# Graph-transformer block on one core: the ends of the two product phases and the last group's row statistics in another order

## Chip, cores and metric

One core of one Trainium2 chip runs the whole kernel. The metric is the device time of one execution in microseconds (us). A profiled execution also leaves a span (first to last instruction) and the clock that the chip granted TensorE, as a share of full speed (1.00 is 2.4 GHz, 0.50 is 1.2 GHz).

## What is computed

The graph has 1250 nodes of 768 features and 40,000 edges of three relations, sorted by target node. With `ln` a layer norm, the block is:

```python
xn = ln(x)
x1 = x + gnn(xn) + mix(xn)
out = x1 + ffn(ln(x1))
```

`gnn` is two relational graph attention layers, the first with four heads of 192 features, the second with one head of 768 and an `elu` between. One layer is:

```python
xr = einsum('nd,rdf->rnf', x, W)            # one product per relation
qi, kj = xr[etype, dst] @ q, xr[etype, src] @ k
alpha = leaky_relu(qi + kj, 0.2)
e = exp(alpha - segment_max(alpha, dst)[dst])
out = segment_sum(e / segment_sum(e, dst)[dst] * xr[etype, src], dst) + b
```

`mix` is linear attention over all nodes with 12 heads, `ffn` an int8 product whose input is rounded to 8 bits after the layer norm.

## The kernel before

Nodes are held in `NB = 10` blocks of 128 rows, padded to 1280. The edges are never gathered. A table `CT` counts, per relation, source node and target node, how many edges there are (built from one-hot products). The attention weight of a pair of nodes is then a dense value, `exp` of a row term plus a column term, cut by a maximum and multiplied by the count; and `segment_sum` is a dense product of this weight table with `xr`.

Every engine has a stream of its own, written by hand in program order, and they meet only at semaphores: `x.wait_ge(sem, n)` holds up everything behind it on that engine. TensorE (`pe`, PE) multiplies, ScalarE (`act`, ACT) and VectorE (`dve`, DVE) make its operands and clear its banks, GpSimd (`pool`, POOL) makes some operands, SyncE (`sp`, SP) issues all loads and stores of this part in one queue. The work goes through these stages:

- **First-layer products** (`product_steps`, L2091 to L2106). `NE = 80` products of 18 matmuls each, 20 for the mix and 60 for `xr` (three relations, two halves, ten blocks). ScalarE evicts each (`xr_part`, L1079) into one of two buffers `ev[j]`, and SP stores it (`store_product`, `store_xr`) into `xr_d` in the chip's memory, 192 KB each. An eviction waits for its buffer's last store. Masks of the edges and the tables of row maxima (`softmax_tables`, `tq`) are made beside it.
- **Head loop** (L2145 to L2170). For each head, relation and source block one *unit*: ScalarE makes `tb` and `vb` (two exponentials of 128x1260 from the broadcast table `qbc`, `pair`, L1152), VectorE makes `vb` (minimum and maximum, L1688) and `pf` (minimum with a bound, times the count, L1692; both in `weights_pair`, L1681), and TensorE multiplies `pf` with the head's features `xrh` (ten matmuls of two passes, L2153). There are 120 units, of which two buffers `pf[0]`, `pf[1]` are in flight. `load_head(g)` brings one head, 2880 KB; `load_table(i)` brings `qbc`.
- **Second layer.** Between the layers come `elu` and transposes. The second products (`m = 0` to 5, ten blocks each) are evicted by ScalarE into `ev2` (L1211) and its low half by VectorE (L1735), stored by `store_x2` into `x2_d`, and read back as `x2[r]`, block by block for `r = 0`. In the trace these buffers show as `x_d` and `x`. `load_q2(g)` brings the table for group `g`.
- **Group loop** (L2199 to L2212). The targets are worked in `NG = 5` groups of 252. A *step* is two source blocks: VectorE makes `v` and `p` (L1762, L1773), ScalarE the high half `ph` (L1226), GpSimd the low half `pl = p - ph` (`p_low`, L946), TensorE multiplies both with `x2[r]`. Each group has 15 steps.
- **FFN** on the rows `fx`, one block of 126 rows at a time. Row statistics (`row_stats`, L1374, on VectorE) and the reciprocal deviation (`rstd_part`, L870, on GpSimd) of eight of the ten blocks are made inside the last group: `stats_of(ss)` gives four blocks each in steps 3 and 4 of relation 1. In relation 2 the first blocks are quantised.

What sets the order around the change is the place of an instruction in its engine's stream. At the end of the first products SP's stream reads, with product `S1 // PM + 4`, number 70 of 0 to 79:

```python
            sp.wait_ge(mt_tr, NW)
            load_head(sp, 0)
            sp.wait_ge(t_step, 14)
            sp.dma_start(tq_d..., tq[0:NW, :, :, :]...).then_inc(tq_st, 16)
            store_product(S1 // PM + 4)
            sp.wait_ge(tq_st, 16)
            load_table(sp, 0)
            for n in range(S1 // PM + 5, NE):
                store_product(n)
```

VectorE and GpSimd enter the head loop behind `wait_ge(g_done, 12 * NB)`, that is when all of these products are done.

## Time and profile before

| | |
|---|---|
| median of 3 runs | 1714.46 us (1712.40 to 1716.67) |
| profiled execution | 1710.97 us, of it span 1709.2 us |
| granted TensorE clock, mean | 0.972 |
| TensorE busy | 1583.9 us (93%), 10783 matmuls |
| TensorE weight loads (beside the matmuls) | 1145.0 us |
| VectorE busy | 1318.3 us (77%) |
| ScalarE busy | 802.4 us (47%) |
| GpSimd busy | 143.3 us (8%) |
| DMA | 178.55 MB, mean 104 GB/s over the span |

One row of a timeline gives the start from the span's beginning, the duration, the engine, the line of the code, the operation with out<-in, and in brackets how long the engine stood idle before and what it waited for. A row of the waits gives what ended the idle time of an engine: total, number of times, longest. In a window, busy times stand in the order TensorE, its weight loads, VectorE, ScalarE, GpSimd. The granted clock is part of each stretch, so a matmul is longer where it is lower.

### The profile page before, as it was taken

What the parts mean: (1) busy time and instruction counts of PE and PEld (TensorE: products, weight loads), DVE (VectorE), ACT (ScalarE), POOL (GpSimd) and SP (SyncE); (2) the same over time, 40 slices, a digit from 0 to 9 for tenths busy, and PEclk for the clock granted to TensorE, in tenths of its full rate; (3) what the DMA queues carried; (4) which work ended last, traced back from release to release, by engine and by line L of the source; (5) the groups of instructions that cost most, each with busy time, mean ns of one, the idle gap of its engine ahead of it and who ended that gap; (6) DMA issues with size and microseconds to landing.
All of it is one profiled execution on the core that took longest, in us unless ns stands there. A gap on an engine that the chain in (4) does not pass through costs nothing.

```text
span 1709.2 us, 34956 instructions
## 1 busy us (share of the span) xinstructions
PE 1583.9 (93%) x10783; PEld 1145.0 (67%) x10784; DVE 1318.3 (77%) x2641; ACT 802.4 (47%) x1065; POOL 143.3 (8%) x260
## 2 busy tenths in 40 slices
PE   3999998988999999789999999989999799999987
PEld 2566675766556666489999999976555455555544
DVE  8699878999489998088898998972783377777785
ACT  4332114542235654178888888862222233333342
POOL 3000000000000000000000000000000133333340
PEclk8999999999999999989999999989999899999999
DMA  5111115520457663540023033033764621011212
GB/s 188 47 58 59 63 32 182 166 79 28 137 185 221 193 203 100 156 139 31 31 70 113 31 113 104 12 101 95 207 204 142 229 83 55 15 40 55 78 45 91
DMA packets 129214, 178.55 MB, mean 104 GB/s; under 512 B 15429, under 2 KB 100526, under 8 KB 129122
## 3 DMA queue, kind: packets, MB, share of 16 engines
q1 hardware_dynamic: 129122, 177.38, 33.1%
q8 instruction: 51, 0.84, 0.2%
q14 instruction: 41, 0.34, 0.1%
HBM read 120.47 MB, written 56.88 MB: 104 GB/s over the span
## 4 chain that ended last, share of the span: by engine, by line
PE 77%; DVE 9%; issue 5%; ACT 3%; DMA 2%; DVEq 1%; POOL 1%; SPq 1%; ACTq 0%; POOLq 0%
PE ps L2153 22%; PE ps L2105 13%; PE ps L2211 7%; PE ps L2210 7%; PE ps L1911 5%; PE ps L1913 5%; PE ps L1912 5%; PE ps L1924 4%; PE ps L2016 3%; DVE oh_q L1412 1%; PE ps L2222 1%; PE ps L2088 1%; DMA xr_d<-ev 1%; DVE oh_p L1413 1%; PE ps L1967 1%
## 5 line engine op out<-in xcount | busy, mean ns | idle before, releaser
L2153 PE MATMUL ps<-xrh,pf 128*128 (+1 forms) x2400 | 399.6, 329 | 11.9 <-DVE pf L1692 11.9
L2153 PEld LDWEIGHTS ps<-xrh,pf 128*128 128x128 f32 x2400 | 393.1, 191 | 18.5 <-issue 16.5
L1688 DVE SCALAR_TENSOR_TENSOR vb<-vb,tb 128x1260 f32<-128x1260 f32 x120 | 173.0, 1466 | 53.0 <-ACT vb L1162 52.1
L1911 PE MATMUL ps<-w_hi,xt_hi 128*128 128x384 f16 x600 | 198.6, 331 | 15.7 <-issue 8.1
L2210 PE MATMUL ps<-x,ph 128*128 (+1 forms) x600 | 196.2, 327 | 16.5 <-POOL pl L946 10.9
L1692 DVE SCALAR_TENSOR_TENSOR pf<-vb,CT 128x1260 f32<-128x1260 f32 x120 | 175.8, 1468 | 35.1 <-PE ps L2153 35.0
L1912 PE MATMUL ps<-w_lo,xt_hi 128*128 128x384 f16 x600 | 198.2, 330 | 0.0
L1913 PE MATMUL ps<-w_hi,xt_lo 128*128 128x384 f16 x600 | 198.0, 330 | 0.0
L2211 PE MATMUL ps<-x,ph 128*128 (+1 forms) x600 | 197.5, 329 | 0.0
L1412 DVE TENSOR_SCALAR oh_q<-pat,codeT,neg_w 125x630 f16<-125x630 uint16 x420 | 186.8, 445 | 12.0 <-PE ps L1924 7.8
L1162 ACT ACTIVATE vb<-qbc,kcol 128x1260 f32<-128x1260 f32 x120 | 161.0, 1345 | 39.3 <-DVE pf L1692 37.9
L1599 DVE CUSTOM_DVE_ANT_0 tt_junk<-kbc,mb 126x1260 bf16<-126x1260 f32 x120 | 169.1, 1467 | 11.7 <-issue 11.7
L1157 ACT ACTIVATE tb<-qbc,kcol_leak 128x1260 f32<-128x1260 f32 x120 | 159.7, 1343 | 20.5 <-DVE vb L1688 19.0
L1226 ACT ACTIVATE ph<-p 128x252 f16<-128x252 f32 x150 | 61.8, 413 | 163.3 <-PE ps L2211 159.6
L1924 PE MATMUL ps<-oh_q,oh_p 125*128 125x315 f16 x840 | 128.6, 301 | 9.9 <-DVE oh_p L1413 9.5
L946 POOL TENSOR_TENSOR pl<-p,ph 128x252 f16<-128x252 f32 x150 | 112.0, 748 | 223.9 <-ACT ph L1226 212.7
L2105 PE MATMUL ps<-w_hi,xt_hi 128*128 128x384 f16 x360 | 118.5, 329 | 6.7 <-ACT ev L1086 6.7
L2105 PE MATMUL ps<-w_hi,xt_lo 128*128 128x384 f16 x360 | 118.3, 329 | 0.0
L2105 PE MATMUL ps<-w_lo,xt_hi 128*128 128x384 f16 x360 | 118.3, 329 | 0.0
L1924 PEld LDWEIGHTS ps<-oh_q,oh_p 125*128 125x128 f16 x840 | 81.7, 99 | 48.2 <-DVE oh_p L1413 12.3
L1413 DVE TENSOR_SCALAR oh_p<-iota_l,sloT 125x128 f16<-125x128 f16 x420 | 104.9, 250 | 0.0
L1773 DVE SCALAR_TENSOR_TENSOR p<-v,CT 128x252 f32<-128x252 f32 x150 | 69.3, 492 | 45.5 <-ACT v L1218 43.9
(257 smaller groups left out, 2422.9 us busy)
## 6 DMA issues: line engine op xcount, KB each, us to landing
qbc<-tq_d SPq DMA_DIRECT2D x12, 1260.0 KB, 6.4
wst<-in_L_gnn_W SPq DMA_DIRECT2D x60, 192.0 KB, 3.3
xr_d<-ev SPq DMA_DIRECT2D x60, 192.0 KB, 2.1
xrh<-xr_d SPq DMA_DIRECT2D x4, 2880.0 KB, 14.8
x_d<-ev SPq DMA_DIRECT2D x60, 192.0 KB, 2.3
mb_d<-mb SPq DMA_DIRECT2D x30, 310.1 KB
mb<-mb_d SPq DMA_DIRECT2D x30, 310.1 KB
x<-x_d SPq DMA_DIRECT2D x2, 3840.0 KB, 18.9
```

What stands on the lines that cost most here:

```text
L1412: dve.tensor_scalar(oh_q[0:ET, u, :], pat[0:ET, :], codes[:, k:k + 1], neg_w[0:ET, ds(w, 1)], ALU.subtract, ALU.is_equal)
L1599: dve.tensor_tensor_reduce(out=tt_junk[k][0:WK, :], in0=kbc[0:WK, h, :], in1=mb[w % 2][0:WK, :], scale=1.0, scalar=2 * BIG, op0=ALU.subtra ...
L1688: dve.scalar_tensor_tensor(vb[j][:, :], vb[j][:, :], 2.0, tb[j][:, :], ALU.min, ALU.max).then_inc(v_step, 1)
L1692: dve.scalar_tensor_tensor(pf[j][:, 0:ND].rearrange("p (w d) -> p w d", d=WN), vb[j][:, :].rearrange("p (w d) -> p w d", d=WN), 2.0, CT[:, ...
L1911: pe.matmul(ps[:, bank, 0:CW], a_hi, hi[:, k, :], start=(k == 0), stop=False)
L1912: pe.matmul(ps[:, bank, 0:CW], a_hi, lo[:, k, :], start=False, stop=False)
L1913: last = pe.matmul(ps[:, bank, 0:CW], a_lo, hi[:, k, :], start=False, stop=(k == K6 - 1))
L1924: last = pe.matmul(ps[:, bank + q, 0:QH], oh_p[0:ET, u, :], oh_q[0:ET, u, q * QH:(q + 1) * QH], start=start, stop=False, skip_group_check= ...
L2105: mm = pe.matmul(ps[:, 6 + n % 2, 0:CW], a[:, k, i * P:(i + 1) * P], w[:, k, :], start=(q % PM == 0 and c >= C_X), stop=(q % PM == PM - 1))
L2153: mm = pe.matmul(out[b], pf[j][:, b * DB:b * DB + P], x, start=(first and b % 2 == 0), stop=False, skip_group_check=True)
L2210: pe.matmul(ps[:, bank, 0:CW], p, cols(off, off + CW), start=start, stop=False, skip_group_check=True)
L2211: mm = pe.matmul(ps[:, bank + 1, 0:CW + n1], p, cols(off + CW, off + D + n1), start=start, stop=False, skip_group_check=True)
```

## The change

It has three edits.

*End of the first products, start of the head loop.* SP no longer issues `load_head(sp, 0)` ahead of the `tq` store. Six pieces of 480 KB (`load_piece`: one relation, five blocks) follow the stores of products 71 to 76, counted from 0, one behind each. ScalarE makes the four exponentials of the first pair of units behind the evictions of products 74 to 77, into `tb[0]`, `tb[1]` and two new tiles `vb_f`, which lie in the place of the second table `qbc[1]`. VectorE computes this pair once `g_done` is `11 * NB`, not `12 * NB`. SP holds table 1 back until the pair is done (`p_done`), GpSimd writes its constants earlier and in two parts, and TensorE waits for each head's own count (`heads_to`, `one_done`).

*End of the second products.* The blocks of `x2[0]` are loaded two a step during product `m = 4`; before, one a step during 4 and 5. In product 5 SP stores `tq2` and the first pair of blocks before it loads table 0; table 1 is loaded between `x2[1]` and `x2[2]`.

*Last group.* `stats_of(r, ss)` gives two blocks a step: steps 2, 3 and 4 of relation 1 and step 0 of relation 2, before four a step in steps 3 and 4 of relation 1. VectorE's row statistics and GpSimd's `rstd_part` both follow it.

TensorE's stream holds the same matmuls in the same order. Cut to one line of context:

```diff
@@ -232,2 +232,3 @@
         pf = [place(f"pf{j}", [P, ND + 4], F32, 43392 + 5056 * j) for j in range(2)]
+        vb_f = [place(f"vb_f{j}", [P, ND], F32, 105536 + 5056 * j) for j in range(2)]
         he = place("he", [P, NDB, HD + 1], F32, 53760)
@@ -531,2 +532,10 @@
 
+        def load_piece(sp, r, a):
+            sp.dma_start(xrh[0][:, r, a * NB // 2:(a + 1) * NB // 2, 0:HD],
+                         xr_d[0, r, a * NB // 2:(a + 1) * NB // 2, :, :].rearrange("b p n -> p b n")).then_inc(xrh_in[0], 16)
+
+        def heads_to(h):
+
+            return 16 * (h // 2 + 1) + (16 * (2 * R - 1) if h % 2 == 0 else 0)
+
         def bank_of(h, b):
@@ -559,5 +568,6 @@
 
-        def stats_of(ss):
+        def stats_of(r, ss):
 
-            return range(4 * (ss - 3), 4 * (ss - 2)) if ss >= 3 else range(0)
+            b = 2 * (NB // 2 * (r - 1) + ss - 2)
+            return range(b, b + 2) if 0 <= b < NDB - 2 else range(0)
 
@@ -711,3 +721,2 @@
             for j in range(2):
-                sp.wait_ge(ev_out[j], 16 * PW + 16)
                 sp.wait_ge(mb_out[j], 16 * NW // 2)
@@ -715,3 +724,2 @@
             sp.wait_ge(mt_tr, NW)
-            load_head(sp, 0)
             sp.wait_ge(t_step, 14)
@@ -723,2 +731,8 @@
                 store_product(n)
+                k = n - (S1 // PM + 5)
+                if k == 4:
+                    for j in range(2):
+                        sp.wait_ge(ev_out[j], 16 * PW + 16)
+                if k < 2 * R:
+                    load_piece(sp, k // 2, k % 2)
             for j in range(2):
@@ -737,2 +751,4 @@
                         sp.wait_ge(y_exp, (i - 1) * NB)
+                    if i == 1:
+                        sp.wait_ge(p_done, 4)
                     if i >= 1:
@@ -780,3 +796,4 @@
 
-                with sp.Fori(0, NB // 2) as ii:
+                def block_pair(m, ii):
+
                     if M2_0 <= m < M2_0 + 3:
@@ -791,11 +808,18 @@
                         weights_piece2(m + 2, ii)
-                    if m >= M2_0 + 3:
-                        b = NB // 2 * (m - M2_0 - 3) + ii
-                        sp.dma_start(x2[0][:, ds(b, 1), 0:2 * D], x2_d[0, ds(b, 1), :, :].rearrange("b p n -> p b n")).then_inc(x2_in[0], 16)
-                if m == 2 * R - 2:
+                    if m == M2_0 + 3:
+                        for u in range(2):
+                            b = 2 * ii + u
+                            sp.dma_start(x2[0][:, ds(b, 1), 0:2 * D], x2_d[0, ds(b, 1), :, :].rearrange("b p n -> p b n")).then_inc(x2_in[0], 16)
+
+                if m == 2 * R - 1:
                     sp.wait_ge(t_step, 28)
                     sp.dma_start(tq2_d.rearrange("s a (w d) -> w (s a) d", d=WD), tq2[0:NW, :, :, :].rearrange("w s a d -> w (s a) d")).then_inc(tq_st, 16)
+                    block_pair(m, 0)
                     sp.wait_ge(tq_st, 32)
-                    for g in range(2):
-                        load_q2(sp, g)
+                    load_q2(sp, 0)
+                    with sp.Fori(1, NB // 2) as ii:
+                        block_pair(m, ii)
+                else:
+                    with sp.Fori(0, NB // 2) as ii:
+                        block_pair(m, ii)
             for j in range(2):
@@ -805,2 +829,4 @@
                 sp.dma_start(x2[r][:, :, 0:2 * D], x2_d[r].rearrange("b p n -> p b n")).then_inc(x2_in[r], 16)
+                if r == 1:
+                    load_q2(sp, 1)
 
@@ -924,6 +950,14 @@
             last.then_inc(sel_done, 1)
-            pool.wait_ge(g_done, 12 * NB)
+            for j in range(4):
+                pool.wait_ge(oa_out[j], 16 * (2 * NB // 4))
             for j in range(2):
-                pool.memset(xrh[j][:, :, :, HD:HD + 1].rearrange("p r b o -> p (r b) o"), 1.0)
-                pool.memset(pf[j][:, ND:ND + 4], 0.0).then_inc(one_done, 1)
+                pool.wait_ge(mb_out[j], 16 * NW // 2)
+            pool.wait_ge(mk_step, H * NW)
+            pool.wait_ge(mt_tr, NW)
+            pool.wait_ge(g_done, 11 * NB)
+            for j in range(2):
+                pool.memset(pf[j][:, ND:ND + 4], 0.0)
+            pool.memset(xrh[0][:, :, :, HD:HD + 1].rearrange("p r b o -> p (r b) o"), 1.0).then_inc(one_done, 1)
+            pool.wait_ge(g_done, 12 * NB)
+            pool.memset(xrh[1][:, :, :, HD:HD + 1].rearrange("p r b o -> p (r b) o"), 1.0).then_inc(one_done, 1)
 
@@ -953,7 +987,10 @@
                 for r in range(R):
-                    with pool.Fori(1 if g == 0 and r == 0 else 0, NB // 2) as ss:
-                        p_low(g, r, ss)
-                    if g == NG - 1 and r == 1:
-                        for b in range(NDB - 2):
-                            rstd_part(b % 2, NB + b, fmv[:, b, :], frstd[:, b, :], DB)
+                    if g < NG - 1 or r == 0:
+                        with pool.Fori(1 if g == 0 and r == 0 else 0, NB // 2) as ss:
+                            p_low(g, r, ss)
+                    else:
+                        for ss in range(NB // 2):
+                            p_low(g, r, ss)
+                            for b in stats_of(r, ss):
+                                rstd_part(b % 2, NB + b, fmv[:, b, :], frstd[:, b, :], DB)
 
@@ -1125,2 +1162,10 @@
                 xr_part(n)
+                j = n - (NE - 6)
+                if j == 0:
+                    act.wait_ge(qb_in[0], 16)
+                    act.wait_ge(w_lo_done, C_2)
+                if 0 <= j < 2:
+                    act.activation(tb[j][:, :], qbc[0][:, 1, :], ACT.Exp, bias=kcol_leak[:, j, 0:1]).then_inc(y_exp, 1)
+                elif 2 <= j < 4:
+                    act.activation(vb_f[j - 2][:, :], qbc[0][:, 0, :], ACT.Exp, bias=kcol[:, j - 2, R * H:R * H + 1]).then_inc(x_done, 1)
 
@@ -1179,3 +1224,3 @@
                     else:
-                        with act.Fori(0, NB // 2) as ss:
+                        with act.Fori(1 if i == 0 else 0, NB // 2) as ss:
                             pair(i, ss)
@@ -1632,3 +1677,2 @@
 
-            dve.wait_ge(g_done, 12 * NB)
             dve.sem_inc(v_step, 2)
@@ -1680,3 +1724,3 @@
 
-            def weights_pair(i, ss):
+            def weights_pair(i, ss, vb=vb):
 
@@ -1699,3 +1743,6 @@
                     if h == 0:
-                        with dve.Fori(0, NB // 2) as ss:
+                        if r == 0:
+                            dve.wait_ge(g_done, 11 * NB)
+                            weights_pair(0, 0, vb_f)
+                        with dve.Fori(1 if r == 0 else 0, NB // 2) as ss:
                             weights_pair(i, ss)
@@ -1842,11 +1889,10 @@
                             weights_part(g, r, ss)
-                            for b in stats_of(ss) if r == 1 else quantised_in(ss):
-                                if r == 1:
-                                    if b % 4 == 0:
-                                        dve.wait_ge(fx_in[b // 4], 16)
-                                    row_stats(fx[:, b, :], b % 2, NB + b, fmv[:, b, :], DB)
-                                else:
-                                    if b == 0:
-                                        dve.wait_ge(mm_done, U2 + ((NG - 1) * R + 2) * NB + 2)
-                                    quantise(b)
+                            for b in stats_of(r, ss):
+                                if b % 4 == 0:
+                                    dve.wait_ge(fx_in[b // 4], 16)
+                                row_stats(fx[:, b, :], b % 2, NB + b, fmv[:, b, :], DB)
+                            for b in quantised_in(ss) if r == 2 else ():
+                                if b == 0:
+                                    dve.wait_ge(mm_done, U2 + ((NG - 1) * R + 2) * NB + 2)
+                                quantise(b)
                     if r == 0 and g >= 1:
@@ -2142,4 +2188,2 @@
 
-            pe.wait_ge(one_done, 2)
-
             def unit_products(n, h, r, s, j, first):
@@ -2156,3 +2200,5 @@
             for h in range(H):
-                pe.wait_ge(xrh_in[h % 2], 16 * (h // 2 + 1))
+                pe.wait_ge(xrh_in[h % 2], heads_to(h))
+                if h < 2:
+                    pe.wait_ge(one_done, h + 1)
                 if h >= 2:
```

SP's queue around the head's load. `ev` are the eviction buffers, `xrh_188` is `xrh[0]`, `qbc_190` is `qbc[0]`. Before:

```order
L488 DMA xr_d<-ev_144 128x2x192
L529 DMA xrh_188<-xr_d 128x30x192
L718 DMA tq_d<-tq 30x24x42
L488 DMA xr_d<-ev_143 128x2x192
L526 DMA qbc_190<-tq_d 128x2x1260
L488 DMA xr_d<-ev_144 128x2x192
L488 DMA xr_d<-ev_143 128x2x192
L488 DMA xr_d<-ev_144 128x2x192
```

and now:

```order
L489 DMA xr_d<-ev_144 128x2x192
L726 DMA tq_d<-tq 30x24x42
L489 DMA xr_d<-ev_143 128x2x192
L527 DMA qbc_190<-tq_d 128x2x1260
L489 DMA xr_d<-ev_144 128x2x192
L534 DMA xrh_188<-xr_d 128x5x192
L489 DMA xr_d<-ev_143 128x2x192
L534 DMA xrh_188<-xr_d 128x5x192
L489 DMA xr_d<-ev_144 128x2x192
L534 DMA xrh_188<-xr_d 128x5x192
L489 DMA xr_d<-ev_143 128x2x192
L534 DMA xrh_188<-xr_d 128x5x192
```

The load of 128x30x192 is gone from the front; the `tq` store and the table stand behind one store each, and pieces of 128x5x192 alternate with the stores behind them.

ScalarE's stream at the evictions of products 73 to 79 of the first layer, as it is now (before, these seven evictions stood in a row and the exponentials behind them):

```order
L1123 ACTIVATE ev_144<-ps 128x384
L1123 ACTIVATE ev_143<-ps 128x384
L1168 ACTIVATE tb_194<-qbc_190,kcol_leak 128x1260
L1123 ACTIVATE ev_144<-ps 128x384
L1168 ACTIVATE tb_195<-qbc_190,kcol_leak 128x1260
L1123 ACTIVATE ev_143<-ps 128x384
L1170 ACTIVATE vb_f_198<-qbc_190,kcol 128x1260
L1123 ACTIVATE ev_144<-ps 128x384
L1170 ACTIVATE vb_f_199<-qbc_190,kcol 128x1260
L1123 ACTIVATE ev_143<-ps 128x384
L1123 ACTIVATE ev_144<-ps 128x384
```

The two `tb` and the two `vb_f` (here `_198`, `_199`) now stand between evictions.

VectorE's stream in the last group, from the `p` of relation 1's step 3 on before, and of its step 2 now. `stat`, `fmv` are the row statistics of `fx`. Before:

```order
L1773 SCALAR_TENSOR_TENSOR p_0_210<-v_0_208,CT 128x252
L1773 SCALAR_TENSOR_TENSOR p_1_211<-v_1_209,CT 128x252
L1377 BN_STATS stat<-fx 126x6 x2
L1379 MEMSET tick 128x1
L1380 BN_AGGR fmv<-stat 126x2
L1377 BN_STATS stat<-fx 126x6 x2
L1379 MEMSET tick 128x1
L1380 BN_AGGR fmv<-stat 126x2
L1377 BN_STATS stat<-fx 126x6 x2
L1379 MEMSET tick 128x1
L1380 BN_AGGR fmv<-stat 126x2
L1377 BN_STATS stat<-fx 126x6 x2
```

and now:

```order
L1820 SCALAR_TENSOR_TENSOR p_0_212<-v_0_210,CT 128x252
L1820 SCALAR_TENSOR_TENSOR p_1_213<-v_1_211,CT 128x252
L1422 BN_STATS stat<-fx 126x6 x2
L1424 MEMSET tick 128x1
L1425 BN_AGGR fmv<-stat 126x2
L1422 BN_STATS stat<-fx 126x6 x2
L1424 MEMSET tick 128x1
L1425 BN_AGGR fmv<-stat 126x2
L1809 TENSOR_SCALAR v_0_210<-qb_0_208,kcol_leak 128x252
L1811 SCALAR_TENSOR_TENSOR v_0_210<-qb_0_208,kcol,v_0_210 128x252
L1809 TENSOR_SCALAR v_1_211<-qb_0_208,kcol_leak 128x252
L1811 SCALAR_TENSOR_TENSOR v_1_211<-qb_0_208,kcol,v_1_211 128x252
```

Two blocks stand between steps where four did, and the next step's `v` follows them.

## Rows read from the trace of the kernel before

**Rows 1.** Page, part 1 (busy us, share, instructions) and clock of part 2.
```profile
PE 1583.9 (93%) x10783; PEld 1145.0 (67%) x10784; DVE 1318.3 (77%) x2641; ACT 802.4 (47%) x1065; POOL 143.3 (8%) x260
...
PEclk8999999999999999989999999989999899999999
```

**Rows 2.** Waits of TensorE, 695 to 745 us: in total, times, longest.
```profile
PE ps L2153 <- DVE pf L1692: 8.8, 1, 8.8
PE ps L2105 <- ACT ev L1086: 6.7, 2, 5.1
```

**Rows 3.** Waits of TensorE, 1315 to 1360 us.
```profile
PE ps L2210 <- DMA x<-x_d: 5.6, 1, 5.6
PE ps L1911 <- DVE ev L1735: 4.4, 1, 4.4
```

**Rows 4.** Waits of TensorE, 1612 to 1675 us.
```profile
PE ps L2210 <- POOL pl L946: 8.2, 5, 4.2
```

**Rows 5.** Timeline of SP's queue, 668 to 745: start, us, line, transfer.
```profile
687.72 0.36 SPq L529 DMA_DIRECT2D xrh<-xr_d  x1
688.13 6.67 SPq L718 DMA_DIRECT2D tq_d<-tq  x1
```

**Rows 6.** Timeline of ScalarE, 668 to 745: start, us, operation, idle before.
```profile
690.82 0.49 ACT L1086 ACTIVATE ev<-ps 128x384 f32<-128x384 f32 x1 [2.44 <-PE ps L2105]
...
723.33 0.49 ACT L1086 ACTIVATE ev<-ps 128x384 f32<-128x384 f32 x1 [2.44 <-PE ps L2105]
```

**Rows 7.** Windows: busy us of PE, PEld, DVE, ACT, POOL; PEclk, DMA, GB/s.
```profile
259.80:262.00 2.20, 2.20 (x25) 1.48 (x26) 1.93 (x5) 2.02 (x4) 1.15 (x3) 0.50 1.02 376
1616.00:1624.00 8.00, 8.00 (x51) 4.79 (x50) 6.51 (x14) 2.79 (x9) 2.35 (x4) 1.00 0.91 342
1633.30:1637.20 3.90, 3.81 (x24) 2.34 (x24) 3.73 (x16) 0.00 (x0) 3.59 (x10) 1.00 0.00 0
```

**Rows 8.** Chain of waits, 650 to 860: start, us, what.
```profile
732.00 100.62 PE ps L2153 x600
```

**Rows 9.** Page, part 6: transfer, count, KB each, us to landing.
```profile
qbc<-tq_d SPq DMA_DIRECT2D x12, 1260.0 KB, 6.4
```

**Rows 10.** Timeline of VectorE, 668 to 745.
```profile
730.38 2.85 DVE L1692 SCALAR_TENSOR_TENSOR pf<-vb,CT 128x1260 f32<-128x1260 f32 x2
...
737.92 1.47 DVE L1692 SCALAR_TENSOR_TENSOR pf<-vb,CT 128x1260 f32<-128x1260 f32 x1 [1.64 <-PE ps L2153]
```

**Rows 11.** Timeline of TensorE, 259 to 262 and 1623 to 1665.
```profile
259.79 0.17 PE L1987 MATMUL ps<-qk_hi,wt_hi 128*128 128x8 f16 x1 [3.12 <-DVE wt_lo L1509]
...
1633.39 0.33 PE L2210 MATMUL ps<-x,ph 128*128 x1 [1.91 <-POOL pl L946]
...
1637.16 0.33 PE L2211 MATMUL ps<-x,pl 128*128 x1
1641.68 0.48 PE L2210 MATMUL ps<-x,ph 128*128 128x384 f16 x1 [4.19 <-POOL pl L946]
```

**Rows 12.** Timelines of ScalarE and GpSimd, 1285 to 1400.
```profile
1319.22 0.49 ACT L1211 ACTIVATE ev<-ps 128x384 f16<-128x384 f32 x1 [2.43 <-PE ps L1913]
...
1348.89 0.49 ACT L1211 ACTIVATE ev<-ps 128x384 f16<-128x384 f32 x1 [2.43 <-PE ps L1913]
...
1350.83 1.46 POOL L946 TENSOR_TENSOR pl<-p,ph 128x252 f16<-128x252 f32 x2 [31.05 <-ACT ph L1226]
```

**Rows 13.** Timeline of VectorE, 1605 to 1650.
```profile
1620.50 1.05 DVE L1773 SCALAR_TENSOR_TENSOR p<-v,CT 128x252 f32<-128x252 f32 x2 [0.74 <-ACT v L1218]
...
1625.41 1.00 DVE L1377 BATCH_NORM_STATS2 stat<-fx 126x6 f32<-126x384 f32 x2
...
1632.38 1.01 DVE L1377 BATCH_NORM_STATS2 stat<-fx 126x6 f32<-126x384 f32 x2
...
1636.95 0.30 DVE L1762 TENSOR_SCALAR v<-qb,kcol_leak 128x252 f32<-128x252 f32 x1
```

2 lines of the change are left out of this document (1 added, 1 removed).

## Prediction

> **What bounds the kernel now.** I read the page first: TensorE is busy for 1583.9 of 1709.2 us, and its granted clock is in the top tenth nearly everywhere [rows 1]. So time comes back only where TensorE stands still or runs slowly, and the reader should look for such places next to the edits. The waits of TensorE show three. Around the end of the first layer's products it waits 8.8 us for the first weights `pf` and 6.7 us for evictions [rows 2]. At the end of the second layer's products it waits 5.6 us for a load and 4.4 us for an eviction [rows 3]. In the last group of the second layer it waits 8.2 us in five pieces for `pl` [rows 4]. The engine and queue timelines then say what each wait hangs on.
>
> **Edit 1, end of the first product.** Before, the 2880 KB load of head 0 is issued at 687.72, and everything behind it in SP's queue is late: the issue of the next store alone takes 6.67 us [rows 5]. The evictions wait for their buffers' stores. ScalarE evicted one product per 2.93 us (0.49 + 2.44) up to 690.82; eight more would have ended at 690.82 + 8 x 2.93 = 714.3, but the last one starts at 723.33 [rows 6]. That is 9.1 us: 6.7 idle, the rest, as I take it, a spell at the lower clock behind it. After the change the load comes in six pieces of 480 KB, one behind each of six stores. A product then brings 192 + 480 KB = 0.69 MB per 2.93 us, 235 GB/s, where a busy stretch carried 342 GB/s [rows 7]. I cost the pieces at nothing for that reason; what hides them is that third of the rate left over, and if it goes, evictions are late again (rival 1). The sixth piece is issued at about 706.3 and has 8 us to land. **Gain 9.1 us**; bounds 0 and 9.1.
>
> The product of the weights moves too. Before, from the last eviction (723.33) to the first matmul of the head loop (732.00 [rows 8]) run two pairs of exponentials, two minima and the first `pf`: 8.67 us. Now ScalarE makes the four exponentials of the first pair behind the evictions of products 74 to 77, each about 1.35 us in a 2.44 us hole, so no eviction is late. ScalarE's new wait for the table sits in front of evictions 75 to 79, which PE waits for. The table goes out once `tq` has been stored, at 688.5 to 692, and takes 6.4 us [rows 9]: 695 to 698.5, against product 74's eviction at 699.6. The fourth exponential ends at 710.2, and one minimum and one product of 1.47 us each put `pf0` at 713.2, 1 us before TensorE is free. So unit 0 starts at 714.3 with no wait and units 0 and 1 fill until 720.8: 30 units take 100.62 us [rows 8], unit 0 of them about 5.85 since VectorE's next `pf` waits for it until 737.92 [rows 10], the others (100.62 - 5.85) / 29 = 3.27. The 8.67 us chain now starts at 714.3 and feeds **unit 2**, at 722.9; TensorE idles 2.1 us in between. Before, unit 2 started at 737.85 + 3.27 = 741.1. Everything of edit 1 together: 741.1 - 722.9 = **18.2 us**. It contains the 2.6 us that unit 0 lost at the lower clock. Whether 2.1 us idle brings that clock back is not certain; after 1.91 us idle the granted clock was 1.00 [rows 7, 11], so I charge nothing and keep 2.6 us as a bound. Then VectorE works 2.94 us a unit against TensorE's 3.27, so the lead is kept. The load that is moved stands behind the `tq` store, a store and the table in SP's queue, all three wanted sooner than it. SP's new wait for the first two `pf` (714.6) has only table 1 behind it, wanted at unit 10, 30 us later. GpSimd's new waits have two short memsets behind them and then nothing until the head loop ends. All of these cost nothing while the head loop's own lead of that size stands.
>
> **Edit 2, end of the second product.** Two 756 KB table loads stood in front of the stores of product pair 0, and the eviction at 1319.22 was the last in time: eight intervals to 1348.89 should be 23.4 us and are 29.7 [rows 12]. The first load now goes behind the pair's two stores, where the next store is due in 2.9 us, and the second leaves the stretch. **Gain 6.3 us**, bounds 0 and 6.3. The blocks of `x2[0]` load two per step during product 4, 768 KB and 384 KB of stores in 5.85 us, about 200 GB/s, covered as above. TensorE no longer waits for the last block but for `pl`: two take 1.46 us from 1350.83, so the first is there at 1351.6, where TensorE started at 1354.4 (last eviction 1348.89 plus 5.6) [rows 3, 12]. **Gain 2.8 us**. It still idles 2.8 us. At 3.12 us idle the clock behind it was 0.50 [rows 7, 11], at 1.91 us 1.00; 3.12 is nearer, so I leave the clock loss of about 1.6 us as it is; it is the upper bound's extra. The loads of `x2[1]` and `x2[2]` go out earlier by the same shift; table 1 slips in between and is wanted 60 us later.
>
> **Edit 3, row statistics.** VectorE did four blocks at a time: 1632.38 to 1636.95 is 4.57 us, so two cost 2.28; one step of weights in a dense stretch is 1632.38 - 1625.41 - 4.57 = 2.40 us [rows 13]. A step of TensorE is 1637.16 + 0.16 - 1633.39 = 3.94 us [rows 11], and it starts 1.0 us after VectorE's step ends (1633.39 against 1632.38). With two blocks each, VectorE needs 4.68 against 3.94, so TensorE now loses about 0.8 a step instead of 1.91 and then 4.19. VectorE is free for the first two blocks at 1621.5; the rows of `fx` must have landed. No row says when: not before 1621.5 is of use, and before the change they were read at 1625.41 without a wait. The four transfers of 378 KB and the first 1512 KB load, 3.1 MB at 342 GB/s [rows 7], take 9.1 us, so I take 1623. Then TensorE's steps start at 1628.8, 1633.5, 1638.2 and 1642.9, with idle times of 1.3, 0.8, 0.8 and 0.8 us, and one of 0.3 behind them. Before it was 8.2 us [rows 4], of which I leave 0.7 for the change of groups (1.91 and 4.19 are in it, so the other three waits are 2.1 together), plus some 1.5 us at the lower clock behind the 4.19 (the two waits of edit 1 cost 2.4 so). **Gain** 7.5 + 1.5 - 4.0 = **5.0 us**, bounds 2.7 (landing at 1625.4, 2.3 us later) and 6.6 (no wait, 1.6 earlier). GpSimd's eight pairs of row statistics spread likewise and stop delaying `pl`.
>
> **Sum.** 18.2 + 6.3 + 2.8 + 5.0 = 32.3 us off the profiled execution's 1710.97: 1678.7. The median of the runs is 3.5 us above that execution, so I say 1714.46 - 32.3 = **1682 us**. With the favourable ends of edits 2 and 3 (1.6 and 1.6 more) it is 1679; with the clock loss in edit 1 (2.6) and the late `fx` (2.3), 1687.
>
> **Rivals.** (1) *The transfers are late*, and the ends of both products still stall. A store behind a 480 KB piece, at half of 342 GB/s, takes 4.0 us with it where 2.93 are free; over six products 1.1 us each, 6.6 us, give 1688.6. For it speaks that stores did queue behind loads in both stretches [rows 2, 3], against it that the old loads were six times a piece. The Trainium skill, DMA: Bandwidth & Descriptors, section Bandwidth, asks for transfers of 1 MiB and more and lists 138 GB/s for 64 KB against 341 for 1 MB; a 480 KB piece lies between, and by that rule the time would be this rival's. The trace carried 342 GB/s with transfers of 378 and 1512 KB mixed, so I give it 0.12. (2) *VectorE is simply full in the last group.* The work is only moved, and if the step with statistics costs the two idle times all the same, edit 3 gives 0: 1687. Chance 0.08. (3) *Slower.* The idle places are also TensorE's rests. If 600 us of products and head loop without one made the chip grant less in the 120 units of the head loop (402 us), the gain is gone at a mean clock of 0.925 there (402 / 0.925 is 33 us more); below that point the kernel is slower, at 0.90 by 45 us more: 1727 us. Against it: the slices that lie wholly in that loop show a 9 [rows 1], and its 29 units after the first keep 3.27 us with no rest. Chance 0.03. (4) *The early weights come too late or the edits miss*: nothing but part of edit 2, within 5 us of before. Chance 0.03.
>
> **How the numbers follow.** The forecast, 1677 to 1687, has 0.74. With rivals 1 and 2 and both together (up to 1693) it is 0.94. The range 1676 to 1691 leaves out the far end of these and rivals 3 and 4. The measurement tells about 0.3% (5 us) from no change. Faster 0.94, same 0.03, slower 0.03.
>
> **What would show it.** In the changed profile: evictions of the last ten first-layer products 2.93 us apart; the first head-loop matmul within 0.5 us of the last product, and one wait for `pf` of about 2 us two units later; no wait of an eviction in the last second-layer product; a wait of about 2.8 us for `pl` in place of 5.6 for the load; in the last group four or five waits under 1.5 us. I am wrong if evictions still wait for stores beside the pieces, if the first `pf` is waited for, or if TensorE's clock in the head loop is under 0.98.

## The result, and the profile after

Median 1687.08 us against 1715.57 before, four runs each. One of the new kernel's four, at 3281.23 us, stands apart for a reason that is not known: it is in that median, but not in the ratio of 0.983 (95% interval 0.9803 to 0.9857). The median of the other three is 1685.57. The forecast was 1682, in the range 1676 to 1691. The gain is 28.5 us by the first median, 30.0 by the second and 29 by the ratio, where 32.3 were worked out. The profiled execution has a span of 1683.7 us, 25.5 less than before. Both kernels spread by 8 to 10 us between executions (the 20 runs of before in one comparison went from 1709.5 to 1719.3), so below the profiles are read for where time goes, and the ratios for how much.

The page after and TensorE's waits over the same three stretches answer to [rows 1 to 4]. The page, busy time and granted clock:

```profile
PE 1579.6 (94%) x10783; PEld 1143.5 (68%) x10784; DVE 1318.7 (78%) x2641; ACT 803.2 (48%) x1065; POOL 143.4 (9%) x260
...
PEclk7999999998999999999999999989999999999998
```

TensorE's waits from 650 to 745 us (in total, times, longest):

```profile
PE ps L2197 <- DVE pf L1736: 2.2, 1, 2.2
```

from 1280 to 1350:

```profile
PE ps L2256 <- POOL pl L980: 2.8, 1, 2.8
```

and from 1580 to 1660:

```profile
PE ps L2256 <- POOL pl L980: 6.7, 6, 3.6
```

The 8.8 and 6.7 us at the end of the first products have become 2.2, the 5.6 and 4.4 at the end of the second have become 2.8, and the 8.2 of the last group are still 6.7. That third line is where the forecast went wrong.

To compare stretches across executions I measure from fixed instructions. `T1` is the eviction of product 71 (690.82 in before, 692.45 in after); `T2` the first matmul of the group loop; `T3` TensorE's matmul behind a wait of 0.62 us in the last group (1615.58 in before, 1589.94 in after), which is where the `fx` loads go out; `T4` the FFN's first matmul with a 2.57 us wait ahead; `T5` the end of the span.

| us | T1 to T2 | T2 to T3 | T3 to T4 | T4 to T5 |
|---|---|---|---|---|
| before | 663.62 | 261.14 | 59.10 | 34.52 |
| after | 636.57 | 260.92 | 57.71 | 36.05 |
| after, profiled again | 637.80 | 262.49 | 57.81 | 35.97 |
| edit 1 alone | 647.17 | 261.21 | 59.20 | 34.47 |
| edit 2 alone | 654.78 | 259.55 | 59.17 | 34.45 |
| edit 3 alone | 663.58 | 261.03 | 55.34 | 34.53 |
| edits 1 and 2 | 638.19 | 260.81 | 58.43 | 34.49 |

From T1 on the changed kernel is 27.1 us shorter. T1 itself came 1.6 us later, with a granted clock of 0.76 in the first 50 us against 0.83, which makes the 25.5 of the span. In the five profiles whose kernels agree up to T2 (the last row, the two of after, and the two further kernels below that change only the last group) T1 to T2 runs from 635.90 to 638.19, so a difference of 2 us in that column says nothing by itself.

**First products.** The chain of waits and VectorE's timeline answer to [rows 8, 10]. The chain (start, us, what):

```profile
680.65 35.10 PE ps L2151 x216
715.75 6.55 PE ps L2197 x40
...
724.51 91.89 PE ps L2197 x560
```

VectorE's timeline:

```profile
713.21 2.85 DVE L1736 SCALAR_TENSOR_TENSOR pf<-vb_f,CT 128x1260 f32<-128x1260 f32 x2
...
722.90 2.84 DVE L1736 SCALAR_TENSOR_TENSOR pf<-vb,CT 128x1260 f32<-128x1260 f32 x2
```

TensorE runs from the products into unit 0 without a stop (680.65 + 35.10 = 715.75), and unit 2's `pf` starts at 722.90. Before, it began unit 2 at 741.1, which is 50.3 us after T1; now it is 724.51 - 692.45 = 32.1 us, 18.2 earlier, just the forecast's 18.2. From 690.0 to 715.7 us, beside the pieces, the DMA engines moved 235 GB/s on average, as much as the forecast had worked out for a store and a piece.

One eviction was nevertheless late, ScalarE's rows:

```profile
695.37 0.49 ACT L1123 ACTIVATE ev<-ps 128x384 f32<-128x384 f32 x1 [2.43 <-PE ps L2151]
699.15 0.49 ACT L1123 ACTIVATE ev<-ps 128x384 f32<-128x384 f32 x1 [3.29 <-DMA xr_d<-ev]
701.22 0.49 ACT L1123 ACTIVATE ev<-ps 128x384 f32<-128x384 f32 x1 [1.58 <-PE ps L2151]
701.61 1.34 ACT L1168 ACTIVATE tb<-qbc,kcol_leak 128x1260 f32<-128x1260 f32 x1
...
715.85 0.49 ACT L1123 ACTIVATE ev<-ps 128x384 f32<-128x384 f32 x1 [2.43 <-PE ps L2151]
```

The eviction at 699.15 waited 3.29 us for the last store of its buffer, some 0.9 longer than the 2.43 of the others, but the next came 2.07 us later and TensorE, with a second bank, never waited. The exponentials fill the holes as costed, 1.34 us in 2.43.

**Second products.** GpSimd's timeline at its first `pl`:

```profile
1328.21 1.46 POOL L980 TENSOR_TENSOR pl<-p,ph 128x252 f16<-128x252 f32 x2 [24.07 <-ACT ph L1271]
```

TensorE's timeline:

```profile
1329.02 0.48 PE L2256 MATMUL ps<-x,ph 128*128 128x384 f16 x1 [2.84 <-POOL pl L980]
```

Two windows, busy times, then granted clock, DMA share and GB/s:

```profile
724.50:728.00 3.50, 3.49 (x21) 3.49 (x22) 3.30 (x3) 3.14 (x3) 0.00 (x0) 1.00 1.10 337
1329.00:1333.00 4.00, 3.98 (x16) 2.01 (x17) 3.21 (x8) 1.24 (x3) 0.80 (x3) 0.64 0.59 152
```

No load is waited for any more; `pl` is, for 2.84 us. In this profile the granted clock is 1.00 behind the 2.23 us of idle time ahead of unit 2 (724.50 to 728), and 0.64 over 4 us behind the 2.84 (1329 to 1333). The last section shows that the second does not hold in every execution.

**Last group.** VectorE and TensorE answer to [rows 11, 13]. VectorE's timeline:

```profile
1594.87 0.97 DVE L1820 SCALAR_TENSOR_TENSOR p<-v,CT 128x252 f32<-128x252 f32 x2 [0.75 <-ACT v L1263]
1599.88 1.02 DVE L1422 BATCH_NORM_STATS2 stat<-fx 126x6 f32<-126x384 f32 x2 [4.05 <-DMA fx<-y_d]
```

SP's queue:

```profile
1589.35 5.42 SPq L849 DMA_DIRECT2D fx<-y_d  x2
```

TensorE:

```profile
1605.54 0.50 PE L2256 MATMUL ps<-x,ph 128*128 x1 [3.63 <-POOL pl L980]
```

VectorE is free at 1595.8 and stands 4.05 us for `fx`, whose load was issued at 1589.35. TensorE then stands 3.63 us for the `pl` behind it, and its next matmuls take 0.50 us each where 0.33 is usual: the granted clock is 0.65 over the next 4 us.

### The profile page after: what moved, and what is told of

Read it like the earlier page. It is cut to its first block, busy times and chain, and to the rows that moved or that the text cites. A ratio compares the mean times of both kernels' runs of the same rounds, so it can differ in the third digit from the quotient of the medians.

```text
span 1683.7 us, 34901 instructions
## 1 busy us (share of the span) xinstructions
PE 1579.6 (94%) x10783; PEld 1143.5 (68%) x10784; DVE 1318.7 (78%) x2641; ACT 803.2 (48%) x1065; POOL 143.4 (9%) x260
## 4 chain that ended last, share of the span: by engine, by line
PE 71%; issue 16%; DVE 8%; ACT 2%; DVEq 1%; DMA 1%; POOL 0%; SPq 0%; POOLq 0%; ACTq 0%
PE ps L2197 22%; PE ps L2151 14%; PE ps L2257 7%; PE ps L2256 7%; PE ps L1970 4%; PE ps L2062 3%; PE ps L1957 2%; PE ps L1958 2%; PE ps L1959 2%; PE ps L2268 1%; DVE oh_q L1457 1%; PE ps L2134 1%; DVE stat L1422 1%; DVE oh_p L1458 1%; PE ps L2013 1%
## 5 line engine op out<-in xcount | busy, mean ns | idle before, releaser
L2197 PEld LDWEIGHTS ps<-xrh,pf 128*128 128x128 f32 x2400 | 390.9, 190 | 11.3 <-issue 8.9
L1970 PE MATMUL ps<-oh_q,oh_p 125*128 125x315 f16 x840 | 127.9, 300 | 10.2 <-DVE oh_p L1458 9.7
L2257 PE MATMUL ps<-x,pl 128*128 (+1 forms) x300 | 98.5, 328 | 0.0
```

What stands on the lines that cost most here:

```text
L1970: last = pe.matmul(ps[:, bank + q, 0:QH], oh_p[0:ET, u, :], oh_q[0:ET, u, q * QH:(q + 1) * QH], start=start, stop=False, skip_group_check= ...
L2197: mm = pe.matmul(out[b], pf[j][:, b * DB:b * DB + P], x, start=(first and b % 2 == 0), stop=False, skip_group_check=True)
L2257: mm = pe.matmul(ps[:, bank + 1, 0:CW + n1], p, cols(off + CW, off + D + n1), start=start, stop=False, skip_group_check=True)
```

## The experiments

Twelve runs followed, of eleven new kernels and the changed one again, in three groups on three chips (the first four, the next four, the last four). The kernel before, run beside each group, had medians of 1712.52, 1712.56 and 1712.15 us, against 1715.57 above. So the ratios to it carry over between groups, and medians do not; where an expectation names a time, the ratio is to be put on 1715.57. The first four runs split the change; the kernel with one edit is the kernel before with that edit's hunks of the diff alone.

**Edit 1 alone.**

> The kernel before with edit 1 alone (pieces of the head's load behind six stores, exponentials and weights of the first pair early). Theory A, the accounting from the two profiles: the edits add up, and edit 1 is worth 18.6 us (head loop ends 16.9 us earlier, and the stretch ahead of the edit had been 1.6 us longer), so about 1697 us against 1715.6. Theory B, the edits lean on each other (later stages lose part of it again, as the last group's wait comes at another moment): less than 15 us, over 1700. In the profile under A: one wait for pf of about 2.2 us two units into the head loop, the last product's eviction to the first unit under 0.3 us.

Median 1694.68, ratio 0.9889 (0.9868 to 0.991): 19 us, theory A. By the table, T1 to T2 falls by 16.5 us. Unit 2 starts 32.1 us after T1 (722.41 - 690.35), as early as in the changed kernel; what is missing from 18.2 lies behind it and is within the spread of that column.

**Edit 2 alone.**

> The kernel before with edit 2 alone (order of transfers at the end of the second products). Theory A: 8.4 us, 6.3 of it the evictions' wait and the rest the load of the last block replaced by the wait for pl; 1707 us. Theory B: under 6 us, 1710 or more. In the profile under A: no wait of an eviction in the last second-layer product, a wait of about 2.8 us for pl at the start of the group loop, and a spell of lower clock behind it.

1704.04, ratio 0.9944 (0.9925 to 0.9964): 9.6 us, theory A; T1 to T2 falls by 8.8. The edits add within the spread: 16.5 + 8.8 = 25.3 against 25.4 with both (663.62 - 638.19).

**Edit 3 alone.**

> The kernel before with edit 3 alone (two blocks of row statistics a step, one step earlier). Theory A, as the two profiles account it: VectorE stands about 4 us for the rows of fx, the last group gains only 1.4 us and the FFN loses 1.5, so 1715.6 within 1.5 us. Theory C, my prediction's price was right and the shortfall lies elsewhere (the start of the kernel, the FFN by chance): 5 us faster, 1710.6. In the profile under A: a wait of TensorE for pl of 3 to 4 us where statistics of the first two blocks are made, and the first fx statistics start about 4 us after their p.

1714.66 (12 runs), ratio 1.0004 (0.9989 to 1.002): nothing that the interval of some 3 us either way can tell. But its profile doesn't show what theory A says: TensorE's longest wait in the last group is 1.7 us. VectorE's timeline:

```profile
1624.60 1.02 DVE L1381 BATCH_NORM_STATS2 stat<-fx 126x6 f32<-126x384 f32 x2 [2.08 <-DMA fx<-y_d]
```

TensorE:

```profile
1630.26 0.33 PE L2213 MATMUL ps<-x,ph 128*128 x1 [1.67 <-POOL pl L947]
```

Here the rows of `fx` landed 8.0 us after T3 (1624.60 - 1616.63), and the last group was 3.8 us shorter, at 1708.24 us for this execution. The runs of this kernel went from 1707.5 to 1718.5. So I take it that what edit 3 brings hangs on a landing time that the median execution doesn't meet; only this one execution was profiled.

**Edits 1 and 2 without 3.**

> The changed kernel with edit 3 undone. Theory A: the same time as the changed kernel within 1.5 us, 1687. Theory C: 5 us slower than it, 1692. The last group should show the waits of before, 1.9 and 4.2 us for pl; whether the FFN's three or four blocks at the lower clock come back as before tells whether its 1.5 us belong to edit 3.

1687.4, ratio 0.9845 (0.9821 to 0.9869): 2.6 us over the changed kernel by the ratios, with intervals that overlap. The last group's two waits are 2.58 and 2.63 us here, not the 1.9 and 4.2 expected. The landing varies here too: in this profile and in that of edit 1 alone, VectorE waited 0.6 and 1.3 us for `fx` even one step later, 10.5 and 11.3 us after T3. The FFN took 34.5 us in all five profiles without edit 3.

**One transfer for six pieces.** (`heads_to` follows, with one count for the load in place of six.)

```diff
                 k = n - (S1 // PM + 5)
-                if k == 4:
-                    for j in range(2):
-                        sp.wait_ge(ev_out[j], 16 * PW + 16)
-                if k < 2 * R:
-                    load_piece(sp, k // 2, k % 2)
+                if k == 0:
+                    for j in range(2):
+                        sp.wait_ge(ev_out[j], 16 * PW + 16)
+                    load_head(sp, 0)
```

> The changed kernel, but head 0 is loaded by one transfer of 2880 KB behind the store of product 71, in place of the six pieces. Tests whether it is the pieces that free the evictions, or already that the load no longer stands ahead of the tq store. Theory A (a large transfer holds up the stores behind it, pieces do not): the evictions of products 73 and on wait for their stores again, 5 to 9 us in all, and the exponentials of the first pair, which stand between evictions, come late with them; 1693 to 1696 us against 1687. Theory R (the place alone counts): no eviction waits over 1 us, 1687.

ScalarE's timeline:

```profile
700.89 0.49 ACT L1122 ACTIVATE ev<-ps 128x384 f32<-128x384 f32 x1 [3.15 <-DMA xr_d<-ev]
710.28 0.49 ACT L1122 ACTIVATE ev<-ps 128x384 f32<-128x384 f32 x1 [8.90 <-DMA xr_d<-ev]
```

SP's queue:

```profile
695.30 0.44 SPq L530 DMA_DIRECT2D xrh<-xr_d  x1
697.76 24.51 SPq L489 DMA_DIRECT2D xr_d<-ev  x7
```

The DMA view from 690 to 724 us (KB, us to landing):

```profile
xrh<-xr_d SPq DMA_DIRECT2D x1, 2880.0 KB, 14.4
```

1689.71, ratio 0.9865 (0.9842 to 0.9889). One eviction waited 8.9 us for the last store of its buffer and TensorE 4.9 us for that eviction; T1 to T2 is 641.95, 4.8 over the mean of the two profiles of after. The load was issued at 695.30 and landed 14.4 us later, at about 709.7; the store issued behind it at 697.76 released the eviction at 710.28. So a store behind a 2880 KB transfer landed only with it. That is theory A; the time, 1692.4 if the ratio is put on 1715.57, falls just short of its 1693. By the profiles the pieces are worth about 5 us, by the ratios 6, with intervals that overlap. The rest of the 9.1 us that edit 1 was to gain on the evictions would then come with the order in the queue, the `tq` store and the table ahead of the load; this was not run by itself.

**The first pair late.** The pieces stay; ScalarE's and VectorE's first pair stand behind the products again.

```diff
-                j = n - (NE - 6)
...
-                if 0 <= j < 2:
-                    act.activation(tb[j][:, :], qbc[0][:, 1, :], ACT.Exp, bias=kcol_leak[:, j, 0:1]).then_inc(y_exp, 1)
...
-                            dve.wait_ge(g_done, 11 * NB)
-                            weights_pair(0, 0, vb_f)
-                        with dve.Fori(1 if r == 0 else 0, NB // 2) as ss:
+                            dve.wait_ge(g_done, 12 * NB)
+                        with dve.Fori(0, NB // 2) as ss:
```

> The changed kernel with the six pieces, but the first pair's exponentials and weights back behind the products, as before. By the sum of the prediction edit 1 is 9.1 us for the evictions and the rest, 18.2 - 9.1 = 9.1, for the early pair; so 9 us slower than the changed kernel, 1696, with one wait for pf of 8.8 us ahead of unit 0 and none ahead of unit 2. If the early pair only moves the 8.8 us chain by two units (6.5 us) and the rest came from the clock, the price is 6.5 us, 1693.5.

TensorE's timeline, the start of the head loop:

```profile
723.62 2.59 PE L2188 MATMUL ps<-xrh,pf 128*128 128x193 f32 x7 [8.76 <-DVE pf L1728]
```

1693.48, ratio 0.9894 (0.9873 to 0.9916), 8 us over the changed kernel's 1685.57 and 1685.29 by the medians and 11 by the ratios, with an interval of some 4 us either way. T1 to T2 is 644.36, 7.2 us over the mean of the two profiles of after. The profiles give the early pair about 7 us, which would be the chain of 8.7 moved by two units of 3.27, with little from the clock; the ratios don't exclude the 9.1 of the forecast.

**Pairs unit by unit.**

```diff
+                for j in range(2):
+                    act.wait_ge(v_step, n + j + 1)
+                    act.activation(tb[j][:, :], qbc[i % 2][:, 1, :], ACT.Exp, bias=sub(kcol_leak, 2 * ss + j)[:, a:a + 1]).then_inc(y_exp, 1)
+                    act.wait_ge(p_done, n + j + 1)
+                    act.activation(vb[j][:, :], qbc[i % 2][:, 0, :], ACT.Exp, bias=sub(kcol, 2 * ss + j)[:, R * H + a:R * H + a + 1]).then_inc(x_done, 1)
...
+                            (weights_by_unit if r == 0 else weights_pair)(i, ss)
```

> The changed kernel with the pairs of head 0, relation 0 (from the second pair on) made unit by unit: ScalarE tb0, vb0, tb1, vb1, VectorE vb0, pf0, vb1, pf1. The chain behind the last eviction is then two exponentials and two VectorE operations, 1.35 x 2 + 0.2 + 1.47 x 2 = 5.8 us, and pf of unit 2 is there when TensorE ends unit 1: the wait of 2.2 us goes, 1685. If the unit-by-unit order costs VectorE's lead later in the loop (a wait for pf in pairs 2 to 4), the gain is under 1 us, 1686 to 1688.

VectorE's timeline:

```profile
716.69 1.47 DVE L1756 SCALAR_TENSOR_TENSOR vb<-vb,tb 128x1260 f32<-128x1260 f32 x1 [2.84 <-ACT vb L1204]
718.30 1.47 DVE L1759 SCALAR_TENSOR_TENSOR pf<-vb,CT 128x1260 f32<-128x1260 f32 x1
```

`pf` of unit 2 ends at 719.8, before TensorE ends unit 1 (713.38 + 6.55 = 719.9), and TensorE has no wait over 0.35 us before 746.8, where it is 0.48. 1680.55, ratio 0.9821 (0.9802 to 0.9839). T1 to T2 is 633.95, 3.2 us under the mean of the two profiles of after. The median fell by 5 us against the changed kernel's 1685.57, but by the ratios it is 1.5, with intervals that overlap; put on 1715.57, the ratio gives 1684.9, the 1685 expected.

**The `fx` load in two.**

```diff
-                sp.dma_start(fx[0:DB, 4 * q:4 * q + 4, :], y_d.rearrange("(b p) n -> p b n", p=DB)[:, 4 * q:4 * q + 4, :]).then_inc(fx_in[q], 16)
+                for f0, f1, k in (((0, 2, 0), (2, 4, 1)), ((4, 8, 2),))[q]:
+                    sp.dma_start(fx[0:DB, f0:f1, :], y_d.rearrange("(b p) n -> p b n", p=DB)[:, f0:f1, :]).then_inc(fx_in[k], 16)
...
-                                if b % 4 == 0:
-                                    dve.wait_ge(fx_in[b // 4], 16)
+                                if b in (0, 2, 4):
+                                    dve.wait_ge(fx_in[b // 2], 16)
```

> The changed kernel with the first load of fx (four blocks, 1512 KB) split into two of two blocks, each with a semaphore of its own. Theory D: edit 3 gains little because the first rows of fx land 9.9 us after the anchor (TensorE's short wait in step 1 of relation 1) where they are wanted at 6; half the bytes land some 2 to 3 us earlier, VectorE's wait of 4.05 us falls under 1.5, TensorE's wait of 3.6 under 1.9 and its spell at the lower clock goes: 3 to 4 us faster, 1683.5. Rival: the transfers around it (loads of ac, stores of y, 1.5 MB) set the landing and not its own size: no change, 1687.

VectorE's timeline:

```profile
1594.46 1.02 DVE L1423 BATCH_NORM_STATS2 stat<-fx 126x6 f32<-126x384 f32 x2 [1.86 <-DMA fx<-y_d]
```

TensorE:

```profile
1600.12 0.33 PE L2257 MATMUL ps<-x,ph 128*128 x1 [1.44 <-POOL pl L981]
...
1604.84 0.33 PE L2257 MATMUL ps<-x,ph 128*128 x1 [0.60 <-POOL pl L981]
```

The first two blocks are there 7.7 us after T3 in place of 9.9. VectorE waits 1.86 us, where under 1.5 was expected, and TensorE 1.44; its matmuls behind that wait keep 0.33 us, so the clock stays up. T3 to T4 falls from 57.7 to 55.1. 1681.43, ratio 0.982 (0.9804 to 0.9836), 1.7 us under the changed kernel by the ratios, with intervals that overlap.

**The changed kernel again**, as the baseline of the last three.

> The changed kernel again, unedited, as the baseline on the same chip for the other three. 1685 to 1688. Its FFN stretch tells whether the 36.05 us seen in the first profile (34.5 in five others) belong to the kernel or vary from one execution to the next: theory V, they vary, 33 to 36 here too.

1685.29, ratio 0.9832 (0.9805 to 0.9859). The last group repeats: VectorE waits 4.22 us for `fx`, 10.1 after T3. So does the FFN, 35.97, where theory V wanted it to vary.

**The split without edit 3.**

> Edits 1 and 2, not 3, with the first fx load split in two as in the run before. A control: if edit 3 needs the early rows of fx to pay (theory D), then the split alone, with four blocks a step and one step later, gains at most the 0.6 to 1.3 us that VectorE waited there, 1686 to 1687, and the last group still shows about 1.9 and 4.2 us of waits. If the split pays by itself, 1683, as with edit 3.

TensorE's timeline in the last group:

```profile
1606.42 0.33 PE L2254 MATMUL ps<-x,ph 128*128 x1 [1.92 <-POOL pl L980]
...
1614.71 0.48 PE L2254 MATMUL ps<-x,ph 128*128 128x384 f16 x1 [4.19 <-POOL pl L980]
```

1684.59, ratio 0.9839 (0.9812 to 0.9865). The two waits of before are there again, T3 to T4 is 60.6, 5.5 us over the kernel with edit 3 and the split (4.0 if the 59.1 of before is taken, which is 1.5 less for the same waits). In the profiles this speaks for theory D. So does the time: 0.9839 of 1715.57 is 1687.9. But its interval, 4.5 us either way, all but reaches the 1683 of the other case, and the 3.3 us by the ratios between this kernel and edit 3 with the split lie within intervals that overlap.

**The group loop's first pair early.**

```diff
                     if m == 2 * R - 1:
                         exp_v(0, 0, 0)
-                    x2_hi(m, NB // 2 - 1)
-            p_hi(0, 0, 0)
+                        x2_hi(m, NB // 2 - 1, (0,))
+                        p_hi(0, 0, 0)
+                        x2_hi(m, NB // 2 - 1, (1,))
```

VectorE's `p` (`p_count(0, 0, 0)`) stands between its last two `x2_lo` in the same way.

> The changed kernel with the first pair of the group loop (p, ph, pl) made between the last two evictions of the second products, in place of behind them. TensorE's wait of 2.84 us for pl goes and the lower clock behind it (0.5 to 1.5 us): 3 to 4 us faster, 1683; if step 1 of the loop is late in its place (its ph waits behind the last eviction), a wait of about 1 us appears there and the gain is 2.

TensorE's timeline at the start of the group loop:

```profile
1327.57 0.32 PE L2262 MATMUL ps<-x,ph 128*128 128x384 f16 x1
...
1332.49 0.33 PE L2262 MATMUL ps<-x,ph 128*128 x1 [0.84 <-POOL pl L980]
```

The wait is gone at 1327.57 and one of 0.84 us stands in step 1, as in the second case expected. T1 to T3 is 895.8 us, against 896.5 to 900.3 in the five profiles named under the table. 1683.74, ratio 0.9835 (0.9808 to 0.9862), no difference that these rounds can tell from the baseline's.

**All three together.**

> The changed kernel with all three further edits: pairs of head 0, relation 0 unit by unit (2.5 us by the profiles), fx load split (2.6 us in the last group, and what the clock gives), first group pair early (3 us). They lie in three different stages, so they should add: 8 us, 1678 or ratio 0.977 to before; TensorE's waits in 700 to 1660 us without one over 1.5 us except the two around the FFN.

1673.89, ratio 0.977 (0.9745 to 0.9795), 11.4 us under the changed kernel run beside it by the medians and 10.6 by the ratios, with intervals that do not overlap; 8 us, or a ratio of 0.977, was expected. It is the fastest of the study. T1 to T2 is 631.23, T3 to T4 54.94.

## Why the prediction was right, and where it was off

**Edit 1 was right in size.** Predicted 18.2; measured 16.5 (profile of it alone) to 19 (ratio). Evictions and unit 0 followed the plan, the 2.1 us idle ahead of unit 2 was 2.23 and cost no clock. How it splits is known less well. The early pair was costed at 9.1 (the chain shift 6.5 and the clock behind the old wait 2.6) and gave about 7 by the profiles and 11 by the ratios; by the profiles pieces and order then gave 9 to 10 for the forecast's 9.1. Edits 1 and 2 together were to bring 27.3 us; T1 to T2 fell by 25.4 to 27.7 in the five profiles of both.

**Edit 2 was right.** Predicted 6.3 + 2.8 = 9.1; measured 8.8 and 9.6. The 2.84 us of idle time is the forecast's 2.8.

**Edit 3 failed.** Predicted 5.0 with bounds 2.7 and 6.6; by the ratio of it alone nothing, in the full kernel 2.6 us with overlapping intervals (0.983 against 0.9845), and 1.3 us in its own stretch. The step that failed is "so I take 1623" for the landing of `fx`, 7.4 us after T3. I worked it out as 3.1 MB at 342 GB/s: the two `ac` loads, the two `y_d` stores of 378 KB each and the first half of `fx`. In the changed kernel's profile the four go out at 1586.2 to 1587.9 and the first half at 1589.35. The second half of `fx`, which the sum left out, goes out at 1594.5, 5.4 us before the first half lands at 1599.9. SP's queue:

```profile
1586.24 0.75 SPq L841 DMA_DIRECT2D ac<-acc_d  x2
1587.03 0.83 SPq L567 DMA_DIRECT2D y_d<-ot  x2
```

The DMA view from 1585 to 1610 us, traffic and issues:

```profile
DMA packets 1598, 4.67 MB, mean 187 GB/s; under 512 B 84, under 2 KB 84, under 8 KB 1596
...
fx<-y_d SPq DMA_DIRECT2D x2, 1512.0 KB
ac<-acc_d SPq DMA_DIRECT2D x2, 378.0 KB
y_d<-ot SPq DMA_DIRECT2D x2, 378.0 KB
```

From the first of these issues to the landing (window as before, GB/s last):

```profile
1586.24:1599.88 13.64, 13.02 (x80) 7.66 (x79) 8.34 (x18) 4.77 (x12) 4.77 (x7) 1.00 0.83 277
```

So 4.6 MB share the queues in place of 3.1. Up to the landing 13.64 us at 277 GB/s moved 3.8 MB, and the landing came 2.5 us later than I took. As an estimate, 0.7 MB more at 342 GB/s is 2.0 us of it; a mean rate under 342 is the rest. The landing also varies. In the nine profiles with edit 3, VectorE's first row statistics and the last group go together:

| run | first statistics, us after T3 | T3 to T4 |
|---|---|---|
| all three together | 7.6 | 54.9 |
| `fx` load in two | 7.7 | 55.1 |
| edit 3 alone | 8.0 | 55.3 |
| first pair late | 8.8 | 56.5 |
| after | 9.9 | 57.7 |
| pairs unit by unit | 10.0 | 57.7 |
| after, profiled again | 10.1 | 57.8 |
| group loop's pair early | 10.2 | 57.9 |
| one transfer for six | 11.3 | 59.4 |

Each us of landing costs about 1.2 us, and at 11.3 nothing is left of the gain (59.1 before). The two divided loads are the two earliest, but edit 3 alone came within 0.3 us of them with an undivided one; why the undivided load lands anywhere from 8.0 to 11.3 is open. The rest of edit 3's sum held: with the landing at 7.7, near my 7.4, TensorE's waits for `pl` with the load in two are 1.44, 0.60, 0.53, 0.54, 0.90 and 0.59, 4.6 us together, where I had 4.0 and 0.7 for the change of groups, and the gain is 4.0 of 5.0.

That the rows "were read at 1625.41 without a wait" (9.8 after T3) was no bound to trust either: two profiles without edit 3 landed at 10.5 and 11.3. With 9.9 VectorE is late by 2.5 us more than I took. That is about the landing of my lower bound, 1625.4, and yet the gain is under its 2.7: TensorE's wait is 3.6 us where I had 1.3, and behind it comes a spell at the lower clock (0.65 over 4 us, 1.4 us lost) that the bound did not hold. The gain in T3 to T4 is 59.1 - 57.8 = 1.3 us, and 1.5 us more in the FFN, at the lower clock, take it back in both profiles of after.

**The FFN** was in no term. In all five profiles without edit 3 it took 34.5 us from T4; in the nine with it 33.2 once, 34.5 three times and 36.0 five times. TensorE's wait ahead is 2.57 us in all of them. What differs is how long the clock is down behind it, in windows of 4 us from T4 (the granted clock is the third number from the end). Before:

```profile
1674.68:1678.68 4.00, 4.00 (x13) 2.36 (x14) 3.86 (x8) 1.62 (x2) 0.00 (x0) 0.57 0.41 141
1678.68:1682.68 4.00, 4.00 (x30) 2.78 (x28) 3.40 (x7) 2.28 (x3) 0.00 (x0) 1.00 0.43 149
```

After:

```profile
1647.65:1651.65 4.00, 4.00 (x18) 2.65 (x19) 3.86 (x8) 1.62 (x2) 0.00 (x0) 0.71 0.41 141
1651.65:1655.65 4.00, 4.00 (x15) 2.16 (x14) 2.98 (x6) 2.54 (x3) 0.00 (x0) 0.50 0.43 149
```

Unit by unit:

```profile
1641.42:1645.42 4.00, 3.86 (x23) 2.57 (x24) 3.86 (x8) 1.62 (x2) 0.00 (x0) 1.00 0.41 141
1645.42:1649.42 4.00, 4.00 (x27) 2.61 (x24) 3.93 (x9) 2.54 (x4) 0.00 (x0) 1.00 0.43 149
```

0.57 and 1.00, then 0.71 and 0.50, then 1.00 and 1.00. The same stop costs 0, 1.3 or 2.8 us. Why edit 3's kernels so often get the long spell was not tried; that it goes with the edit is what 5 and 9 profiles show, no more.

**The rivals.** Rival 1 (evictions late beside the pieces) shows as one eviction of 0.9 us delay, without effect; at 2880 KB in one transfer it is true. The Trainium skill's rule of 1 MiB and more per transfer (DMA: Bandwidth & Descriptors, section Bandwidth) did not decide here: six pieces of 480 KB went through without a wait of TensorE, where one transfer of 2880 KB cost it 4.9 us. Rival 2 (edit 3 gives nothing, 1687) came close in number, by another mechanism: not because VectorE is full, since with early rows the same distribution took T3 to T4 down by 3.8 us (edit 3 alone) and 5.5 (with the split load, against the split without edit 3). Rival 3 (lower clock in the head loop) is refuted: the granted clock (third from the end) is 1.00 over it, where under 0.98 was to be the sign.

```profile
716.00:1108.00 392.00, 387.20 (x2341) 380.81 (x2340) 347.20 (x288) 334.52 (x261) 0.00 (x0) 1.00 0.23 72
```

Rival 4 (early weights too late) is refuted too: unit 0 follows the last product without a wait.

So the time fell in the upper part of the range, which "landing at 1625.4" and rival 2 had put there. That this was enough is in part luck. The landing was a term of that part (2.3 us); the 1.4 us of clock behind it and the 1.5 in the FFN were in no term, and fitted in because the 2.6 us of clock held back for edit 1 were not used.

## What to carry to other kernels

When a consumer is moved earlier, the transfer it reads becomes a term of its own: take its landing from all bytes that are in the queues until it lands, those issued behind it too, and from several profiles; and split it so that the first rows come first. A wait of zero in one profile bounds nothing until several profiles show it. And when a chain can't be hidden whole, make the first item's part of it short (unit by unit, not pair by pair) and let the work already prepared cover it.
